# Clamping the recurrence's exponents on ScalarE and re-staging the norm, the mask and the scans of a four-stage gated block

## What is computed

```
x = x + tanh(g_xattn[0]) * attention(layernorm(x), mask, ctx)         # 32 heads of 8, rope, plus an adapter of 64 keys
x = x + tanh(g_ffn[0])   * top1_experts(layernorm(x))                 # 8 experts of 256x256
x = x + tanh(g_xattn[1]) * wkv(w, u, k=layernorm(x), v=ctx)           # recurrence over the 64 tokens
x = x + tanh(g_ffn[1])   * top2_experts(layernorm(x))                 # 8 experts, 704 wide, silu

def step(carry, kv_t):                                                # the recurrence, per sequence and feature
    p, q, o = carry
    no = max(o, u + kt);  A = exp(o - no);  E = exp(u + kt - no)
    y = (A * p + E * vt) / (A * q + E)
    no2 = max(w + o, kt); A2 = exp(w + o - no2); E2 = exp(kt - no2)
    return (A2 * p + E2 * vt, A2 * q + E2, no2), y
```

## Time and profile before

| what | us |
|---|---|
| median of 3 runs | 589.53 |
| lowest and highest | 589.38, 597.02 |
| the profiled execution | 592.08 |
| its span, first to last instruction | 590.3 |
| PE busy | 507.2 (86%) |
| DVE busy | 331.3 (56%) |
| ACT busy | 217.4 (37%) |
| POOL busy | 147.6 (25%) |

### The profile page before, as it was taken

The page is one execution under the profiler, slowest core; times in us unless marked ns, Lnnn a source line. Parts: engine busy times, 40 slices in busy tenths (PEclk is TensorE's granted clock), DMA queues, the critical chain, the costliest instruction groups (busy, mean ns, idle before and its releaser), DMA issues.

```text
span 590.3 us, 10170 instructions
## 1 busy us (share of the span) xinstructions
PE 507.2 (86%) x3131; PEld 364.0 (62%) x3132; DVE 331.3 (56%) x945; ACT 217.4 (37%) x478; POOL 147.6 (25%) x228
## 2 busy tenths in 40 slices
PE   1587999898998998989979567688899999999994
PEld 0365767676676675766757445455577676667662
DVE  5552578888897888978865857636411111111110
ACT  1717365273562644627412222421122222222221
POOL 3070113213123131131211150310424333433322
PEclk9757998999999999999958679888899999999998
DMA  8700000000000000000000659799512112212211
GB/s 219 218 1 6 2 6 2 2 24 2 5 19 1 22 0 4 18 0 24 2 4 19 268 212 397 250 393 415 175 19 37 27 27 36 36 22 31 36 18 18
DMA packets 19136, 44.48 MB, mean 75 GB/s; under 512 B 5688, under 2 KB 15424, under 8 KB 17440
## 3 DMA queue, kind: packets, MB, share of 16 engines
q1 hardware_dynamic: 13824, 37.50, 17.5%
q0 software_dynamic: 4416, 6.03, 6.3%
q10 hardware_dynamic: 864, 0.54, 0.3%
HBM read 38.30 MB, written 5.24 MB: 74 GB/s over the span
## 4 chain that ended last, share of the span: by engine, by line
PE 52%; DVE 22%; issue 13%; ACT 4%; POOL 4%; DMA 3%; SPq 1%; DVEq 1%; POOLq 0%; ACTq 0%
PE bank_s L1681 18%; PE bank_o L1712 9%; PE bank_t L1583 4%; DVE X L1008 2%; PE bank_s L1490 2%; PE bank_b L1701 2%; PE bank_o L1539 2%; DVE ND L1048 2%; DMA CT<-in_ctxT 2%; PE bank_a L1552 2%; POOL rstd L476 2%; DVE mx L952 1%; DVE st L883 1%; PE bank_t L1520 1%; PE bank_c L1450 1%
## 5 line engine op out<-in xcount | busy, mean ns | idle before, releaser
L1681 PE MATMUL bank_s<-wr_all,xgT 128*128 x288 | 89.1, 463 | 0.0
L1243 DVE TENSOR_TENSOR hh<-sg,bank_s 128x352 f32<-128x352 f32 x46 | 24.0, 521 | 88.4 <-PE bank_s L1681 76.6
L1681 PEld LDWEIGHTS bank_s<-wr_all,xgT 128*128 128x128 f32 x288 | 53.9, 192 | 27.1 <-issue 0.7
L474 POOL TENSOR_SCALAR rstd<-mv 128x1 f32<-128x1 f32 x32 | 7.2, 224 | 202.9 <-DVE mv L886 202.9
L952 DVE TENSOR_REDUCE mx<-bank_s 128x8 f32<-128x512 f32 x64 | 43.6, 688 | 24.1 <-PE bank_s L1492 22.3
L1712 PE MATMUL bank_o<-wr_all,hT 128*128 x216 | 53.2, 388 | 0.7 <-DVE hT L1237 0.7
L1490 PE MATMUL bank_s<-Kh,Qx 128*128 128x128 f32 x256 | 45.5, 305 | 5.7 <-ACT Qx L642 5.7
L556 POOL DMA_INDIRECT out_x<-ys,idx_out x18 | 28.9, 1603 | 75.7 <-ACT ys L808 75.7
L1712 PEld LDWEIGHTS bank_o<-wr_all,hT 128*128 128x128 f32 x216 | 38.2, 189 | 10.8 <-issue 6.9
L1490 PEld LDWEIGHTS bank_s<-Kh,Qx 128*128 128x128 f32 x256 | 39.6, 215 | 8.5 <-issue 6.6
L1237 DVE COPY hT<-bank_c 128x256 f32<-128x256 f32 x23 | 9.7, 423 | 62.4 <-PE bank_c L1701 62.4
(11 more groups left out here) (316 smaller groups left out, 1013.4 us busy)
## 6 DMA issues: line engine op xcount, KB each, us to landing
wr_all<-in_w SPq DMA_DIRECT2D x8, 2176.0 KB
e<-in_w SPq DMA_DIRECT2D x5, 1408.0 KB, 8.1
e<-in_w SPq DMA_DIRECT2D x5, 768.0 KB, 7.4
CT<-in_ctxT SPq DMA_DIRECT2D x1, 1024.0 KB, 9.8
Pt<-in_WT SPq DMA_DIRECT2D x1, 1024.0 KB
mrow<-mhl SPq DMA_DIRECT2D x64, 8.0 KB, 1.9
X<-in_x SPq DMA_DIRECT2D x1, 896.0 KB, 6.8
out_x<-X SPq DMA_DIRECT2D x6, 128.0 KB, 1.7
```

What stands on the lines that cost most here:

```text
L1243: dve.tensor_tensor(hh[:, i * IH:(i + 1) * IH], sg[:, i, :], bs[1][:, 0:IH], ALU.mult).then_inc(h_in, 1)
L1681: ins = pe.matmul(bs[k][:, 0:IH], xgT[:, c, :], w(c, 2 * i + k), start=(c == 0), stop=(c == KT - 1))
```

## The change

1. The eight clamps leave DVE. ACT does them in `clamp(u)`, as Relu with a bias per feature: max(d + w, 0) as before, and max(-(d + w), 0) = -min(d + w, 0) with scale -1 and the negated column `nwc` (new, one DVE instruction at the start); likewise with u. The exp of `EX` gets scale -1. A new semaphore `clamped` ties clamp to decay, and the next tile's `dd` waits for it.
2. On ACT, clamp stands behind both exps of `attend(t, 2)`, and decay behind the `heads_out(t, 1)` that follows; before, decay stood ahead of `attend(t, 2)`.
3. The low part of the mask is subtracted by POOL, right behind its copy.
4. Norm 0 of tile t+2 is computed at the end of round t (statistics in place of `mask_low`, apply behind `low_k`), not that of t+1 at the start of round t; on POOL `rstd_of(0, t+2)` stands ahead of the products. Tile 1's norm moves ahead of the rounds.
5. On DVE the scans stand behind the next tile's unit 0 of the maxima, ahead of its unit 1; before, ahead of both.
6. The loop runs over pairs instead of steps of two.

```diff
+        def two_on(t, nxt):
+
+            return nxt and not (isinstance(t, int) and t == NT - 2)
...
             def mask_of(t, par):
                 after(pool, t_mm, t - 2, 8, 8)
                 pool.tensor_copy(mk2[par][:, :, 0:S], MK[:, bass.ts(t, BT), :]).then_inc(mk_hi, 1)
+                after(pool, mk_hi, t, 1, 1)
+                pool.tensor_tensor(mk2[par][S:P, :, 0:S], MK[S:P, bass.ts(t, BT), :], mk2[par][S:P, :, 0:S].bitcast(F32),
+                                   ALU.subtract).then_inc(mk_in, 1)
+                after(pool, mk_in, t, 1, 1)
...
-                if nxt and prev:
-                    rstd_of(0, t + 1)
...
                     rstd_of(2, t - 1)
+                if two_on(t, nxt):
+                    rstd_of(0, t + 2)
...
+            def clamp(u):
+                after(act, arg_in, u, 1, 1)
+                after(act, dec_exp, u - 1, 3, 3)
+                for c in range(KT):
+                    for i, col, neg in ((0, wc, nwc), (1, nuc, uc)):
+                        act.activation(AR[:, 0, i, c, :], dd[:, c, :], ACT.Relu, scale=-1.0, bias=neg[:, c:c + 1])
+                        ins = act.activation(AR[:, 1, i, c, :], dd[:, c, :], ACT.Relu, bias=col[:, c:c + 1])
+                ins.then_inc(clamped, 1)
+
             def decay(u):
-                after(act, arg_in, u, 1, 1)
-                act.activation(EX[:, :, :, :], AR[:, 0, :, :, :], ACT.Exp).then_inc(dec_exp, 1)
+                after(act, clamped, u, 1, 1)
+                act.activation(EX[:, :, :, :], AR[:, 0, :, :, :], ACT.Exp, scale=-1.0).then_inc(dec_exp, 1)
...
                 if nxt:
                     evac_kT(t + 1, 1 - par)
+                attend(t, 2)
+                if prev and nxt:
+                    clamp(t - 1)
+                heads_out(t, 1)
                 if prev and nxt:
                     decay(t - 1)
-                attend(t, 2)
-                heads_out(t, 1)
                 attend(t, 3)
...
                 if prev and not nxt:
+                    clamp(t - 1)
                     decay(t - 1)
...
             scaled(0)
+            clamp(u)
             decay(u)
...
-            def mask_low(t, par):
-                after(dve, mk_hi, t, 1, 1)
-                dve.tensor_tensor(mk2[par][S:P, :, 0:S], MK[S:P, bass.ts(t, BT), :], mk2[par][S:P, :, 0:S].bitcast(F32),
-                                  ALU.subtract).then_inc(mk_in, 1)
...
             def wkv_args(u):
-                link(dve.tensor_tensor(dd[:, :, :].rearrange("p c (b s) -> p (c b) s", b=BT), Op[:, :, 0:S], kk[:, :, :], ALU.subtract))
-                for c in range(KT):
-                    for i, col in ((0, wc), (1, nuc)):
-                        dve.tensor_scalar(AR[:, 0, i, c, :], dd[:, c, :], col[:, c:c + 1], 0.0, ALU.add, ALU.min)
-                        ins = dve.tensor_scalar(AR[:, 1, i, c, :], dd[:, c, :], col[:, c:c + 1], 0.0, ALU.add, ALU.max)
-                ins.then_inc(arg_in, 1)
+                after(dve, clamped, u - 1, 1, 1)
+                dve.tensor_tensor(dd[:, :, :].rearrange("p c (b s) -> p (c b) s", b=BT), Op[:, :, 0:S], kk[:, :, :], ALU.subtract).then_inc(arg_in, 1)
...
+            ln_stats(0, 1)
+            ln_apply(0, 1)
             dve.tensor_scalar(nuc[:, :], uc[:, :], -1.0, None, ALU.mult).then_inc(prep, 1)
+            dve.tensor_scalar(nwc[:, :], wc[:, :], -1.0, None, ALU.mult).then_inc(prep, 1)
...
-                if nxt:
-                    ln_stats(0, t + 1)
                 maxima(t, range(2, 3))
-                if nxt:
-                    ln_apply(0, t + 1)
...
                     rotate_k(t + 1, 1)
-                    mask_low(t + 1, 1 - par)
+                if two_on(t, nxt):
+                    ln_stats(0, t + 2)
...
                 if nxt:
                     low_k(t + 1, 1 - par)
+                if two_on(t, nxt):
+                    ln_apply(0, t + 2)
+                if prev2:
+                    after(dve, h4_out, w, 16, 16)
+                if nxt:
+                    maxima(t + 1, range(1))
                 if prev and nxt:
                     wkv_scans(u)
-                if prev2:
-                    after(dve, h4_out, w, 16, 16)
                 if nxt:
-                    maxima(t + 1, range(2))
+                    maxima(t + 1, range(1, 2))
```

26 lines of the change are left out of this document (13 added, 13 removed).

## The result

The changed kernel took 601.47 us (median of 4 runs, 600.43 to 601.94), the kernel before beside it 592.36 (median of 4). The ratio is 1.0141, with a 95% interval of 1.0092 to 1.019: slower, by some 1.4%, and within the 2% that the forecast called no change. It is 10.7 us over the forecast and 0.5 beyond the upper end of its range (601). The profiled execution took 601.64 with a span of 599.8, against 592.08 and 590.3.

A forecast was written before the change was run, and what follows sets the result against it. No engine is full; handovers bound the kernel, mostly on DVE, at tile ends through ACT and POOL. +1.6 - 0.7 + 0.3 = +1.2 on 592.08 gives 593.3, less 2.55 for the median: 590.8 us, range 583 to 601.

The forecast's parts named there:

- Clamps on ACT: Eight clamps at each tile's end on ACT: 0.28 us apart, 2.24 us per tile, bounds 0.20 to 0.35 each.
- The new end of a tile: From attend(t, 2)'s end on PE to the reciprocal opening heads: 8.45 us against 8.89, so 0.44 earlier.
- POOL under heads: DVE's heads multiplications held until POOL's sums end: 0.7 us per tile, bounds 0 and 2.05.
- Per tile +0.26: Each tile end: -0.44 for the earlier reciprocal, +0.7 for POOL's hold; +1.6 us over six tile ends with scans.
- the one that I had called dearer: The last of six tile ends with scans, dearer for having no norm to lose; let cancel against the first.
- The start: Tile 1 loses 0.44 us of hn ahead of heads, first tile's norm 0 gains little: -0.7 in all.
- Behind the last tile: gi 1.57 us earlier without tile 6's clamps on DVE; last tile's silu 1.9 later behind ACT's clamps: net +0.3.
- TensorE's clock falls: Rival: PE's longer waits at tile ends halve its clock, 2.5 us in five tiles, 12.5 in all, 603; chance 0.12.
- the bounds on ACT and POOL: Range terms: clamps at 0.20 to 0.35 give -4.5 to +4 us, the hold on heads -4.2 to +8.1.

The follow-up runs named there:

- the kernel moved by 19: Changed kernel with 19 instructions that only wait for what is there, put ahead of the loop on DVE; 597.68 us (one run).
- both maxima first: Changed kernel with both first maxima of the next tile ahead of the scans on DVE; 602.66 us, ratio 1.017.
- changed, wide: Changed kernel with two waiting instructions ahead of DVE's loop and four matmuls of 512 columns per tile around groups 2 and 3; 596.02 us, ratio 1.0065.
- PE kept busy: Changed kernel with three matmuls of 512 columns between a tile's last value product and unit 3's row scores; 599.08 us, ratio 1.0101.
- the kernel with the norm alone: Kernel before with only attention's norm a tile further ahead and the loop form it needs; 592.02 us, ratio 0.999.

## Why the prediction was off

The forecast (590.8, no change) was 10.7 too low; of this, 2.8 is the reference itself: the median of three runs was 589.53, that of the four beside the result 592.36. Against the latter the forecast's +1.2 stands against +9.1 measured. By its steps:

- *Clamps on ACT*, 0.28 apart, 2.24 per tile: 0.29 apart, 2.34 from the first to `Oc`. Right. The estimate from the figures of the page "ScalarE: Activation LUTs" of the Trainium skill, section "What ACT_TABLE_LOAD costs", 0.29 and 2.35, was a hair nearer than my own interpolation.
- *The new end of a tile*, 8.45 from the end of `attend(t, 2)` to the reciprocal: 8.26. Right in its terms; ACT's VE is what the scans wait for (1.78 us).
- *POOL under heads*, +0.7 per tile: right in the one tile worked through, `heads(u, 0)` takes 2.33 (223.71 to 226.04) against 1.63 before, from its start at 219.22 to the next maximum. With POOL idle, behind the stall, it takes 1.64. The hold ended with POOL's sums (225.16) and not with its list (226.92).
- *Per tile +0.26*, +1.6 in all: about right at a full clock. Both with wide matmuls, the five tiles together are 2.0 longer in the changed kernel (190.07 against 188.04), one fall and 0.5 us per tile of further wide matmuls included. The dearer tile was the one that I had called dearer.
- *The start*, -0.7: the first reciprocal came 0.3 sooner, and the tile behind it was 1.7 shorter at a clock of 1.00 against 0.95.
- *Behind the last tile*, -1.57 and +1.9. The gain has to show ahead of the last reciprocal, since the clamps of tile 6 stood ahead of it; the last tile was 2.2 shorter (39.07 against 41.28), part of it the clock's (0.83 against 0.74), and 1.1 at a like clock (0.75, the kernel moved by 19). The loss was mis-sized: the tail grew by 3.9. `ys` to `sg` grew by 2.07 against the kernel with these clamps on DVE, near to the 1.9, but their removal gave back 2.9 us. The first gather issued 2.98 behind the reciprocal as before (343.12 and 337.50), but PE got its rows another 1.0 later, which the sum didn't have.
- *TensorE's clock falls*: here the step that failed is that the clock stays at 1.00 in the loop. The fall was a rival with 0.12 of the chance, priced at 2.5 us in each of five tiles, 12.5 in all. It happened in every tile of the loop. It cost 0.7 to 1.4 us per tile in the changed kernel (38.7 to 39.2 against 37.6 to 38.0), next to nothing in two tiles of the kernel moved by 19 (37.76 and 37.55 at 0.95), and two falls in one tile cost 3.8. I had weighed it by PE's waiting time, since 1.67 us went with a clock of 0.53 and 1.23 with 1.00 (the window of the earlier trace rows ends before that wait; those behind it show 1.00 too). The runs speak against that: a fall without a gap (both maxima first), no fall with a wait of 1.81 (changed, wide), a fall and none behind the same 1.92 (PE kept busy), and most falls gone when the narrow stretch gets wide matmuls. The spread of the kernel before (589.38 and 597.02 in the three runs shown) should have told me that the clock falls more often in some of its runs. Its one trace shows no fall in the loop's tiles; that the spread is falls there rests on the mean clocks and on the runs with wide matmuls.
- *Not in the prediction at all*: the stall at the branch back, 4.64 us at its place and 3.8 in the time, the largest single part. Moving code ahead of a loop was costed at its own run time only.

Put together by runs: 601.5 as changed; 597.7 without the stall; 594.8 without the last tile's clamps on ACT as well; and 593.5 to 594.0 the kernel before, as the median of 13 to 25 runs beside each batch. What is left, about 1 us, is the difference of several things that no run takes apart: the slower gathers and the falls in every tile against what the change gained elsewhere. The profiled executions give the parts by stage:

| stage (us, changed less before) | forecast | measured |
|---|---|---|
| up to the second reciprocal (105.40 before) | -0.4 | -2.0 |
| the five tiles behind it | +1.3 | +9.8, of it 4.6 the stall and 5.2 with the clock at 0.89 to 0.95 |
| the last tile | -1.6 | -2.2 |
| behind it | +1.9 | +3.9 |
| sum | +1.2 | +9.5 |

So three steps failed: the stall that wasn't there, the clock in the tiles, and the size of the term for the tail. The range nearly reached to the time only by the bounds on ACT and POOL, which had no share in it; that was luck, and so is it that the time stayed within 2%.

Still open is why the stretch lets the clock fall in every tile of the changed kernel and only in some of the others. PE's order is the same in all kernels without added matmuls. What differs is when it comes to the stretch, and what stood ahead: PE waited 0.80 for `Pt` before the wide matmuls of `attend(t, 3)` in the kernel before, and doesn't in the changed one. No run separates the two.

## What to carry to other kernels

Before weighing a change on a tuned kernel, look at the spread of its runs beside their mean clock: and where the two go together, at the stretch in which the clock falls. Here two useless wide matmuls in it took 4.3 us off the kernel before, and no part of the rewrite was seen to gain as much. When a loop's program changes, look for idle time put down to the issue at its branch back, and at the packets on the engine's instruction queue, before blaming the algorithm. And work that is moved ahead of a table load can be paid in full (here 2.07 us of 2.34 at its place), where the same work on another engine ran beside the load.

## What the runs showed of the hardware

- The branch back of a loop of 314 instructions on DVE costs nothing or 4.6 to 4.8 us by where the loop lies in DVE's queue: with its first instruction in place 192 or 193 three kernels have the stall, and 20 packets of 8 KB on the instruction queue; with it in places 195 to 212 the kernel before and ten others (bodies of 314 to 332 instructions) have none, and 15 packets.
- The clock can fall to half while PE is busy without a gap, in narrow matmuls: in the kernel with the norm alone it did so in one tile end and not in the ones beside it, at the same order and the same widths. Two matmuls of 512 columns in that stretch cut the spread of the kernel before from 9.4 us (22 runs) to 4.1 (10 runs).
- Four DVE instructions, two of them multiplications of two SBUF operands, take 2.33 us beside POOL's sums and 1.64 with POOL idle, in one and the same execution.
- The gathers behind the tiles (median of six, from issue to landing) took 4.4 us before, 5.5 in the changed kernel, 5.8 with only the last clamps back on DVE, and 4.0 with all of them back. All eight kernels with the tiles' clamps on ACT have 5.5 to 5.8, and all six with them on DVE 4.0 to 4.4. The page's rows of the changed kernel and of that with the clamps on DVE:

```profile
xg<-normed,gi POOLq DMA_INDIRECT x6, 5.5
```

```profile
xg<-normed,gi POOLq DMA_INDIRECT x6, 4.0
```

What in the clamps' place does it, no run tells: the issue lies at the same distance from the reciprocal, and the cause stays open.
